# Attention on one core: subtraction of the maxima and weighted sums one group later, denominators' work regrouped

## The reference

```
layer 0:  y = groupnorm(x);  q, k, v = qkv_w y + qkv_b
          x = x + proj_w softmax(q k / 8) v + proj_b
layer 1:  h = [x, position embedding];  q = h Wq, k = h Wk, v = x Wv
          x = x + softmax(q k / 8) v Wout + bout
```

## Time and profile before

| | |
|---|---|
| time, median of 3 runs | 4300.96 us (4295.68 to 4301.03) |
| the profiled execution | 4301.96 us, span of its instructions 4300.2 us |
| PE busy | 4097.7 us, 95% of the span |
| DVE busy | 3211.7 us, 75% |
| ACT busy | 2815.7 us, 65% |
| GpSimd busy | 1408.7 us, 33% |
| mean granted PE clock | 0.992 of full speed |

### The profile page before, as it was taken

One profiled execution on the slowest core, in us unless ns is written; L12 is line 12 of the kernel. 1 busy time (PEld: TensorE's weight loads), 2 busy tenths in 40 slices (PEclk: granted clock), 3 DMA queues, 4 the chain that ended last, 5 costly groups with the idle time before them and its releaser, 6 DMA issues. The chain is left out here.

```text
span 4300.2 us, 88739 instructions
## 1 busy us (share of the span) xinstructions
PE 4097.7 (95%) x30024; PEld 1912.0 (44%) x30024; DVE 3211.7 (75%) x4032; ACT 2815.7 (65%) x3557; POOL 1408.7 (33%) x572
## 2 busy tenths in 40 slices
PE   7998999999999999998999989999999999999989
PEld 4554444444444444444555544444444444444445
DVE  3112899999999999997322239999999999999962
ACT  1112788888888888886000018888888888888850
POOL 0000444444444444443100004444444444444410
PEclk9999999999999999999999999999999999999999
DMA  4122000101000000011323320100000000000116
GB/s 173 73 80 86 8 28 18 35 13 31 21 26 22 22 24 24 26 48 41 124 101 124 105 84 9 35 15 31 18 27 24 22 22 24 26 20 29 41 45 212
DMA packets 157934, 208.42 MB, mean 48 GB/s; under 512 B 9009, under 2 KB 144305, under 8 KB 156849
## 3 DMA queue, kind: packets, MB, share of 16 engines
q1 hardware_dynamic: 137712, 179.28, 12.7%
q10 hardware_dynamic: 20160, 28.32, 1.8%
HBM read 113.19 MB, written 94.37 MB: 48 GB/s over the span
## 5 line engine op out<-in xcount | busy, mean ns | idle before, releaser
L589 POOL TENSOR_TENSOR prob<-prob,mx 128x1056 f32<-128x1056 f32 x564 | 1387.7, 2460 | 2675.9 <-DVE prob L589 2675.9
L755 ACT ACTIVATE prob<-psum_att 128x768 f32<-128x768 f32 x1728 | 1393.3, 814 | 967.9 <-PE psum_att L681 539.4
L681 PE MATMUL psum_att<-qst,kst 64*128 64x384 f32 x6912 | 1288.3, 504 | 26.8 <-DMA kst<-qk_scratch 17.9
L692 PE MATMUL psum_att<-prob,vst 128*32 128x384 f32 x13824 | 1239.9, 491 | 77.3 <-ACT prob L771 77.2
L771 ACT ACTIVATE prob<-prob 128x1152 f32<-128x1152 f32 x1152 | 1285.6, 1164 | 0.0
L860 DVE TENSOR_TENSOR run<-psum_att,run 128x768 f32<-128x768 f32 x1344 | 1234.0, 950 | 11.9 <-PE psum_att L681 2.7
L589 DVE TENSOR_TENSOR prob<-prob,mx 128x1248 f32<-128x1248 f32 (+1 forms) x576 | 853.5, 1483 | 65.4 <-ACT mx L763 65.4
L681 PEld LDWEIGHTS psum_att<-qst,kst 64*128 64x128 f32 x6912 | 624.0, 188 | 530.7 <-ACT prob L755 152.3
L692 PEld LDWEIGHTS psum_att<-prob,vst 128*32 128x32 f32 x13824 | 396.1, 109 | 834.9 <-issue 573.3
L872 DVE TENSOR_TENSOR two_tiles<-prob 128x768 f32<-128x768 f32 x564 | 559.0, 991 | 0.4 <-ACT prob L771 0.4
L309 PE MATMUL psum<-xc_l,wq 128*128 128x384 f32 x1536 | 504.0, 489 | 10.1 <-DVE qk_l L406 5.0
(11 more groups left out here) (55 smaller groups left out, 1596.3 us busy)
## 6 DMA issues: line engine op xcount, KB each, us to landing
qk_scratch<-qk_l SPq DMA_DIRECT2D x48, 768.0 KB, 3.5
v_scratch<-vo_l SPq DMA_DIRECT2D x24, 768.0 KB, 3.5
qst<-qk_scratch SPq DMA_DIRECT2D x96, 192.0 KB, 2.4
kst<-qk_scratch SPq DMA_DIRECT2D x96, 192.0 KB, 2.4
vst<-v_scratch SPq DMA_DIRECT2D x96, 192.0 KB, 2.5
att_scratch<-ob ACTq DMA_DIRECT2D x96, 192.0 KB, 1.9
attc_l<-att_scratch SPq DMA_DIRECT2D x24, 768.0 KB, 5.4
x_sb<-in_x SPq DMA_DIRECT2D x8, 1152.0 KB, 13.9
```

The lines of the kernel that those rows point to most:

```text
L589: return engine.tensor_tensor(x, x, m, ALU.subtract)
L681: mm = nc.tensor.matmul(psum[:, 2 * k + e, 0:CH], kst[rows, (3 * c + k) * P:(3 * c + k + 1) * P], qst[par][rows, :], start=True, stop=True ...
L692: mm = nc.tensor.matmul(psum[d:d + 32, 6, 0:CH], vst[:, kt, d:d + 32], prob[par][:, d // D, kt, :], start=(kt == 0), stop=(kt == KT - 1), ...
L755: nc.scalar.activation(prob[par][:, :, s, :], s_banks(k)[:, :, 0:CH], ACT.Copy).then_inc(copied, 1)
```

## The change

The key groups pass the same engines with other lags. The subtraction has lag 8 instead of 7, the weighted sums lag 11 instead of 10. The denominators keep lag 11, so they now stand in the same PE group as the weighted sums of the same keys, and `DEN_LAG` is gone; a new semaphore `weighed` counts the last weighted sums of a block, and `pv_done` counts PE groups from the first denominators on. On ACT the copy of the weighted sums stands between the two exponentials of c=4, and the copy of the denominators right behind the second of them. The turn of the denominators with their sum, inversion and widening moves from c=2 to c=3, their spread, the norms and the store from c=3 to c=4. The core of the diff:

```diff
-SHIFT_LAG, EXP_LAG, PV_LAG, PAIR_LAG, DEN_LAG = 7, 9, 10, 10, 11
+SHIFT_LAG, EXP_LAG, PAIR_LAG, PV_LAG = 8, 9, 10, 11
-PV_COPY_AT, DEN_COPY_AT, DEN_TURN_AT, DEN_SPREAD_AT, STORE_AT = 3, 5, 2, 3, 3
+PV_COPY_AT, DEN_TURN_AT, DEN_SPREAD_AT, STORE_AT = 4, 3, 4, 4
...
                     pe.wait_ge(mx_ready, 3 * (t - 1) + k + 1)
+                if c > BROADCAST_AT + 1 and not live(t) and live(t - 1):
+                    pe.wait_ge(mx_ready, 3 * t)
...
                     tv, pv, cv = behind(t, par, c, PV_LAG)
-                    td, pd, cd = behind(t, par, c, DEN_LAG)
-                    mm = None
                     if live(tv):
-                        mm = weigh(tv, pv, cv)
-                    if live(td):
-                        mm = add_keys(td, pd, cd)
-                    if mm is not None:
-                        mm.then_inc(pv_done, 1)
+                        weigh(tv, pv, cv)
+                        add_keys(tv, pv, cv)
...
                 if not before(t, 2):
-                    act.wait_ge(pv_done, pv_count(t - 2, c + 1))
+                    act.wait_ge(pv_done, pv_count(t - 2, c))
...
             def copy_weighted(t):
-                act.wait_ge(pv_done, pv_count(t, KC - 1))
+                act.wait_ge(weighed, t + 1)
...
             def copy_den(t):
-                act.wait_ge(pv_done, pv_count(t, KC))
+                act.wait_ge(pv_done, pv_count(t, KC - 1))
...
-                    if c == DEN_COPY_AT and not before(t, 2) and live(t - 2):
-                        copy_den(t - 2)
...
                             copy_weighted(t - 2)
+                    if c == PV_COPY_AT and not before(t, 2) and live(t - 2):
+                        copy_den(t - 2)
...
-                    dve.wait_ge(pv_done, pv_count(t, c - 1))
+                    dve.wait_ge(pv_done, pv_count(t, c - 2))
```

More of the change, by code:

```diff
@@ L543, in attention_stage @@
         paired = sem("paired")
-        pv_done = sem("pv_done")
+        weighed, pv_done = sem("weighed"), sem("pv_done")
         den_copied, pv_copied = sem("den_copied"), sem("pv_copied")
@@ L694, in weigh @@
                                               tile_position=(0, d))
-                return mm
+                if c == KC - 1:
+                    mm.then_inc(weighed, 1)
             def add_keys(t, par, c):
@@ L709, in add_keys @@
                                               stop=(c == KC - 1 and (n == len(rounds) - 1 or r % D > 0)), tile_position=(0, r))
-                return mm
+                mm.then_inc(pv_done, 1)
             def body(t, par):
```

## The result

The changed kernel takes 4245.75 us (median of 4 runs, 4244.34 to 4247.07) against 4300.66 (4295.68 to 4301.03): ratio 0.9875 with the interval 0.9858 to 0.9892. That is 55 us faster, where 63 were forecast; the time lies inside the forecast's own range. The profiled execution took 4246.06 us.

A forecast was written before the change was run, and what follows sets the result against it. PE was taken as the fullest engine, its gaps closable only as far as DVE and ACT follow. From 4302, 54 us for steady blocks and 9 for the ends gave 4239, taken as 4238; 8-in-10 range 4195 to 4292, own range 4222 to 4262.

The forecast's parts named there:

- The weighted sums' wait: PE in c=4: the weighted sums' 0.71 us wait for exponentials makes the group 0.79 over; 0.15 won, 0.64 returning before the fold.
- S4: Start of the scores of group c=4 on PE, from which the prediction counts times.
- The turn of the denominators: PE in c=1: this turn waits for the last copy of the maxima; moving it to c=3 wins 0.44 us a block.
- S2: Start of the scores of group c=2 on PE, from which the prediction counts times.
- The steady blocks: Both attention stages, 92 block periods: 0.44 + 0.15 = 0.59 us won in each, 54 us in all.
- every PE wait goes: Rival: with the fold not late, a block loses 1.26 us, 116 us in 92 blocks, giving 4177; chance 0.09.
- the turn of the denominators gains nothing: Rival: late score copies of c=2 leave only 0.15 us a block won, 23 us with the ends, 4279; chance 0.24.
- no gain at all: Rival: the two preceding rivals, plus ACT 0.15 us late at the turn: 4302, less or more the ends; chance 0.07.
- the slower one: Rival: exponentials wait for GpSimd after the later subtraction, delaying score copies; block 0.38 us longer, 4337; chance 0.08.
- the dearer case: GpSimd's subtraction ending 0.34 us later than placed moves DVE's fold by 0.24 a block: 22 us worse, 4260.
- The ends: Fill and drain of both attention stages: together -9 us, between -20 and +12.
- I take -2 per stage: Drain: added weighted sums (about 2 us) and subtraction against waits such as 1.75 us; taken as -2, between -6 and +5.

## Why the prediction was right, and where it was not

**The weighted sums' wait** (0.79): gone, and 0.64 of it came back at the turn of the maxima, as worked out. The fold was placed at S4 + 9.26 and stands at 9.25, the turn at 10.37 and stands at 10.35. That DVE's chain sets it and not ACT's, which was placed 0.1 ahead, is shown by the run with small copies: ACT's last copy came away from the fold's end, and the turn stayed. With small norms the turn moved by the 0.32 that DVE's chain lost; that run alone would not tell the two engines apart, since ACT's last copy moved along (1230.23 against the fold's end at 1230.24): its score copies of c=4 follow maxima that stand between the norms. In the changed kernel the two engines are within 0.01 of each other.

**The turn of the denominators** (0.44): gone. The last score copy of c=2 was placed at S2 + 4.7 and ends at S2 + 4.62. What the prediction had as a side remark, that the subtraction must leave its place at the maxima for the copies of c=2 to be in time, proved to be a condition: without it the gain is nil.

**The steady blocks** together: 92 x 0.59 = 54 forecast, 54.3 measured. The rival that every PE wait goes fell with the fold; that the turn of the denominators gains nothing, with that turn's missing wait, and no gain at all with it; the slower one, with exponentials that don't wait for GpSimd in the blocks.

**GpSimd and the fold**: GpSimd ended 0.08 before the fold, 0.1 was forecast, and the fold took 0.96. So the 22 us of the dearer case did not come, by a tenth of a microsecond. By the prediction's own row that case was a little further off than it says: the pair sum at 1226.28 lost 0.24 to a subtraction that ended 0.38 after the pair sum's start, so GpSimd's end would have had to come 0.48 later than placed for the same loss, not 0.34.

**The ends** are the mis-sized term: -9 forecast, -2.8 measured in fill and drain. The fill was forecast at -2.7 a stage: -2.5 and -1.5. The step "I take -2 per stage" in the drain gave +0.3 and +0.9. It set waits such as 1.75 against the added group of weighted sums by choice instead of a sum. The runs with GpSimd's part made small show equal drains (40.63 and 40.63), so the difference comes with GpSimd's part, and the run with the subtraction at lag 7 shows that it is the later subtraction that brings it, 1.1 and 1.9 us. That step leaves one more GpSimd subtraction behind the last turn. DVE meets it, which the prediction priced (4.80) and did not count; and the exponentials wait for GpSimd, since the score copies that cover this in the blocks are missing there. The prediction said that ACT waits without that cover, and put no price on it in the drain. What each of the two costs is open. DVE in the drain of the changed kernel, and GpSimd beside it:

```profile
1955.11 2.49 DVE L870 TENSOR_TENSOR two_tiles<-prob 128x768 f32<-128x768 f32 x1
...
1959.13 3.25 DVE L870 TENSOR_TENSOR two_tiles<-prob 128x768 f32<-128x768 f32 x1 [0.16 <-ACT prob L769]
...
1964.78 4.81 DVE L589 TENSOR_TENSOR prob<-prob,mx 128x2304 f32<-128x2304 f32 x1
```

```profile
1954.34 2.44 POOL L589 TENSOR_TENSOR prob<-prob,mx 128x1056 f32<-128x1056 f32 x1 [3.35 <-DVE prob L589]
1959.11 2.46 POOL L589 TENSOR_TENSOR prob<-prob,mx 128x1056 f32<-128x1056 f32 x1 [2.33 <-DVE prob L589]
1964.24 2.94 POOL L589 TENSOR_TENSOR prob<-prob,mx 128x1056 f32<-128x1056 f32 x1 [2.67 <-DVE prob L589]
```

Both stretched pair sums end 0.82 and 0.81 after GpSimd's end, nearly their whole undisturbed 0.95, as if they had only begun about then; the large subtraction took 4.81 beside GpSimd and 2.55 in the run where GpSimd's part was small. The Trainium skill (SBUF — State Buffer, Who interferes with whom) says that a VectorE instruction with two SBUF inputs contends with a GpSimd instruction that reads SBUF, under an exclusive lock: this drain agrees with it, at 2.3 us for one meeting (3.25 - 0.95).

## What to carry to other kernels

When a wait is to be removed, compute when the next event would allow the engine to go on: here a fold that allowed the turn at the very moment at which it started took back 0.64 of 0.79, and the list of waits had hardly named it. A move can be worth nothing without another (the turn's alone: nothing; all but the subtraction's: nothing; all together: 55 us), so a group of moves is judged by runs that leave one out. Stages have ends: work shared between two engines in the steady loop may cost time in the drain, where the cover that hid it is missing.

## What was not expected of the hardware

Small instructions save less than their size: a norm on 8 columns took 0.17 us against 0.29 on 128, an ACT copy of 8 columns 0.17 against 0.48 on 384. The meeting of DVE and GpSimd works both ways: GpSimd's subtraction at 1964.24 took 2.94 instead of 2.46, and in the run with small subtractions one on 48 elements a partition took 0.87 (at 1957.02, beside a pair sum on DVE) where the two others of that drain took 0.29.
